# Search rounds that mask two thresholds and fold the masks on TensorE, with identity products in between

## The reference

```python
input_acts_seq = input_acts.mean(axis=1)                              # 64 x 2048
top_input_acts, top_input_idx = jax.lax.top_k(input_acts_seq, 256)
input_repr = zeros.at[brow, top_input_idx].set(top_input_acts)
process_acts = gelu(einsum('bn,pn->bp', input_repr, process_input_weights))
top_process_acts, top_process_idx = jax.lax.top_k(process_acts, 128)  # of 1024
process_weights = softmax(top_process_acts)
aggregated_value = einsum('bk,bkd->bd', process_weights, process_values[top_process_idx])
output_acts_seq = gelu(einsum('bd,od->bo', aggregated_value, output_input_weights))
top_output_acts, top_output_idx = jax.lax.top_k(output_acts_seq, 256) # of 2048
out_per_seq = einsum('bk,bkm->bm', top_output_acts, output_patterns[top_output_idx])
```

## Time and profile before

| | us |
|---|---|
| median of 3 runs | 1627.82 (1626.67 to 1629.48) |
| the profiled execution | 1629.22 |
| its span, first to last instruction | 1627.5 |
| `route` in the span | 1402 to 1627.5 |
| rounds of stage 1 | 1407.9 to 1460.5 |
| rounds of stage 2 | 1527.4 to 1579.2 |

### The profile page before, as it was taken

The page is one execution under the profiler, slowest core; times in us unless marked ns, Lnnn a source line. Parts: engine busy times, 40 slices in busy tenths (PEclk is TensorE's granted clock), DMA queues, the critical chain, the costliest instruction groups (busy, mean ns, idle before and its releaser), DMA issues. The chain is left out here.

```text
span 1627.5 us, 31837 instructions
## 1 busy us (share of the span) xinstructions
PE 1473.0 (91%) x9736; PEld 1380.4 (85%) x9736; DVE 967.6 (59%) x2424; ACT 946.6 (58%) x3359; POOL 116.9 (7%) x243
## 2 busy tenths in 40 slices
PE   5899999999999999999999999999999998774431
PEld 4799999999999999999999999999999998772330
DVE  6766655555555555555555655555566643485686
ACT  3566666666666666666666666666666654780440
POOL 0000000000000000000000000000000000000000
PEclk9999999999999999999999999999999999757555
DMA  8311111111111111111111111111110000267007
GB/s 204 80 45 45 45 44 44 42 40 40 43 44 44 44 44 44 44 44 42 39 39 40 39 40 39 39 41 44 44 44 10 10 11 10 85 210 319 0 1 316
DMA packets 53237, 99.36 MB, mean 61 GB/s; under 512 B 16720, under 2 KB 35664, under 8 KB 52176
## 3 DMA queue, kind: packets, MB, share of 16 engines
q1 hardware_dynamic: 50912, 96.91, 20.2%
q10 hardware_dynamic: 2288, 2.00, 0.6%
HBM read 73.17 MB, written 25.69 MB: 61 GB/s over the span
## 5 line engine op out<-in xcount | busy, mean ns | idle before, releaser
L625 ACT ACTIVATE ffn<-ffn 128x196 f32<-128x196 f32 x1024 | 329.5, 322 | 210.3 <-PE ffn L513 209.8
L513 PE MATMUL ffn<-x_t_hi,pat_w_hi 128*128 128x392 f32 x1024 | 361.8, 353 | 1.7 <-DVE x_t_lo L780 1.7
L513 PE MATMUL ffn<-x_t_hi,pat_w_lo 128*128 128x392 f32 x1024 | 349.5, 341 | 0.0
L513 PE MATMUL ffn<-x_t_lo,pat_w_hi 128*128 128x392 f32 x1024 | 349.0, 341 | 0.0
L716 DVE SCALAR_TENSOR_TENSOR shared<-shared,gen 98x512 f32<-98x512 f32 x64 | 44.0, 687 | 279.3 <-ACT shared L598 279.3
L513 PEld LDWEIGHTS ffn<-x_t_hi,pat_w_hi 128*128 128x128 f32 x1024 | 193.0, 188 | 6.1 <-DVE x_t_lo L780 2.0
L513 PEld LDWEIGHTS ffn<-x_t_lo,pat_w_hi 128*128 128x128 f32 x1024 | 193.6, 189 | 1.2
L625 ACT ACTIVATION_READ_ACCUMULATOR ffn<-ffn 128x1 f32 x1024 | 193.6, 189 | 0.0
L513 PEld LDWEIGHTS ffn<-x_t_hi,pat_w_lo 128*128 128x128 f32 x1024 | 192.9, 188 | 0.0
L443 PE MATMUL gen<-qkvu_w_hi,h_t_hi 128*98 128x512 f32 (+1 forms) x512 | 173.3, 338 | 2.0 <-ACT q_t L580 2.0
L443 PE MATMUL gen<-qkvu_w_hi,h_t_lo 128*98 128x512 f32 (+1 forms) x512 | 172.5, 337 | 0.0
(11 more groups left out here) (219 smaller groups left out, 2768.2 us busy)
## 6 DMA issues: line engine op xcount, KB each, us to landing
raw<-in_x_dram SPq DMA_DIRECT2D x752, 56.0 KB, 2.0
h_dram<-h SPq DMA_DIRECT2D x128, 98.0 KB
process_nat<-ocess_input_weights_dram SPq DMA_DIRECT2D x8, 1024.0 KB, 4.9
process_t<-h_dram SPq DMA_DIRECT2D x8, 896.0 KB, 11.9
out_dram<-process_t SPq DMA_DIRECT2D x8, 896.0 KB, 6.3
h_early<-h_dram SPq DMA_DIRECT2D x4, 896.0 KB, 12.3
out_dram<-h_early SPq DMA_DIRECT2D x3, 896.0 KB, 3.8
pat_nat<-_ffn_input_patterns_dram SPq DMA_DIRECT2D x1, 2048.0 KB, 15.9
```

Of the source, the lines that this page charges most:

```text
L513: last = pe.matmul(fb[f % FFN_BANKS][:, 0:T2], a[:, d, f * P:(f + 1) * P], b[:, d, :], start=n == 0, stop=n == 3 * s.halves - 1)
L625: last = act.activation(cols, cols, ACT.Gelu, accum_out=gelu_sum[:, par, at:at + 1])
```

## The change

Each round now tries two thresholds on VectorE and one on ScalarE, over all 1024 words each. VectorE no longer sums: four instructions (two thresholds, two halves of 512 words) write masks of zeros and ones in bf16 (L1305). TensorE multiplies each block of 64 mask columns with `image_sum`, now bf16, and adds the 16 blocks of a threshold in PSUM: 32 products of 64 columns a round, which wait for the four masks in turn. ScalarE's signs come in by a product of 64 columns, 63 of which are constants. VectorE then sums the 64 columns of each threshold (L1310) before it judges, so that there is one more instruction between TensorE and the judgement. In stage 2 five identity products follow each round's sums. In the ranking 24 identity products are issued once the tenth of the 16 steps is done, ahead of the turning of the ranks.

```diff
-        SHARED_AT = 5 * HALF // 8
-        reached_too = sb("reached_too", [P, 2 * HALF - SHARED_AT], BF16)
+        BLOCK = 64
+        reached_too = sb("reached_too", [P, HALF], BF16)
+        MASKED = HALF // 2
+        MASKS = 2 * HALF // MASKED
...
-        image_sum = sb("image_sum", [P, P], F32R)
+        image_sum = sb("image_sum", [P, P], BF16)
...
             def sum_halves(n):
-                tally = tallies[n % 2][:, 0:4]
                 if n == 0:
                     pe.wait_ge(numbers_made, 1)
-                if n >= 2:
-                    pe.wait_ge(judged, n - 1)
-                pe.matmul(tally, image_sum[:], offset, start=True, stop=False)
+                for m in range(2):
+                    for at in range(0, HALF, BLOCK):
+                        if at % MASKED == 0:
+                            pe.wait_ge(masked, MASKS * n + (m * HALF + at) // MASKED + 1)
+                        pe.matmul(tally[:, m * BLOCK:(m + 1) * BLOCK], image_sum[:], reached[m][:, at:at + BLOCK],
+                                  start=at == 0, stop=at == HALF - BLOCK)
                 pe.wait_ge(counted_too, n + 1)
-                pe.matmul(tally, image_minus_half[:], signs, start=False, stop=False)
-                pe.wait_ge(counted, n + 1)
-                pe.matmul(tally, image_sum[:], count, start=False, stop=True).then_inc(summed, 1)
+                pe.matmul(tally[:, 2 * BLOCK:3 * BLOCK], image_minus_half[:], signs[:],
+                          start=True, stop=True).then_inc(summed, 1)
...
+            pe.wait_ge(copied, fills + out_fills)
+            pe.wait_ge(taken, 2 * (s.k_proc // 8 - 6))
+            keep_busy(24)
             pe.wait_ge(ranks_found, 1)
...
-            pe.wait_ge(copied, fills + out_fills)
             keep_busy(5)
             place_ties(2)
...
             for n in range(STAGE, 2 * STAGE):
                 sum_halves(n)
+                keep_busy(5)
...
-                    act.activation(reached_too[:, 0:HALF], word[:], ACT.Sign, scale=-1.0, bias=tried[:, 4:5],
-                                   accum_out=signs[:, 2:3])
-                    act.activation(reached_too[:, HALF:], word[:, SHARED_AT:], ACT.Sign, scale=-1.0,
-                                   bias=tried[:, 3:4], accum_out=signs[:, 1:2]).then_inc(counted_too, 1)
+                    act.activation(reached_too[:], word[:], ACT.Sign, scale=-1.0, bias=tried[:, 4:5],
+                                   accum_out=signs[:, 0:1]).then_inc(counted_too, 1)
...
-                        for m, cols in enumerate((HALF, SHARED_AT)):
-                            last = dve.tensor_scalar(reached[m][:, 0:cols], word[:, 0:cols], tried[:, 1 + m:2 + m],
-                                                     0.0, ALU.is_ge, ALU.add, accum_out=count[:, m:m + 1])
-                        last.then_inc(counted, 1)
+                    for m in range(2):
+                        for first in range(0, HALF, MASKED):
+                            cols = slice(first, first + MASKED)
+                            dve.tensor_scalar(reached[m][:, cols], word[:, cols], tried[:, 1 + m:2 + m], None,
+                                              ALU.is_ge).then_inc(masked, 1)
...
                     dve.wait_ge(summed, n + 1)
-                    dve.tensor_scalar(passed[:], tallies[n % 2][:, 0:3], float(s.k_in), 0.0, ALU.is_ge, ALU.add,
+                    dve.reduce_sum(counts[:], tally[:, 0:3 * BLOCK].rearrange("p (m b) -> p m b", b=BLOCK),
+                                   axis=AX.X).then_inc(counted, 1)
+                    dve.wait_ge(counted, n + 1)
+                    dve.tensor_scalar(passed[:], counts[:], float(s.k_in), 0.0, ALU.is_ge, ALU.add,
                                       accum_out=found[:]).then_inc(judged, 1)
```

More of the change, by code:

```diff
@@ L945, in route @@
         ahead = sb("ahead", [P, 5])
-        blank = sb("blank", [P, 12])
-        numbers = sb("numbers", [P, 12], F32R)
-        count, signs, offset = (numbers[:, n:n + 4] for n in (0, 4, 8))
-        image_sum = sb("image_sum", [P, P], F32R)
+        blank = sb("blank", [P, BLOCK])
+        signs = sb("signs", [P, BLOCK], F32R)
+        counts = sb("counts", [P, 3])
+        image_sum = sb("image_sum", [P, P], BF16)
         image_minus_half = sb("image_minus_half", [P, P], F32R)
@@ L963, in route @@
         sums = ctx.enter_context(nc.psum_tensor("sums", [P, 512], F32))
-        tallies = [sums, turn[2]]
+        tally = turn[2]
         prod = [ctx.enter_context(nc.psum_tensor(f"rp{b}", [P, 512], F32)) for b in range(4)]
@@ L969, in route @@
         acts_turned, wide_made, chosen = sem("acts_turned"), sem("wide_made"), sem("chosen")
-        words_made, tried_made, numbers_made, counted, counted_too = sem("words_made"), sem("tried_made"), sem("numbers_made"), sem("counted"), sem("counted_too")
+        words_made, tried_made, numbers_made, counted, counted_too, masked = sem("words_made"), sem("tried_made"), sem("numbers_made"), sem("counted"), sem("counted_too"), sem("masked")
         summed, ahead_made, judged = sem("summed"), sem("ahead_made"), sem("judged")
@@ L1041, in _ @@
             pool.wait_ge(masks_made, 5)
-            pool.memset(blank[:, 9:10], (HALF - SHARED_AT) / 2)
-            pool.memset(blank[:, 10:11], HALF / 2).then_inc(masks_made, 1)
+            pool.memset(blank[:, 1:2], float(-HALF)).then_inc(masks_made, 1)
             pool.tensor_tensor(tie_share[:], other_half[:], same_image[:], ALU.subtract).then_inc(masks_made, 1)
@@ L1232, in _ @@
             act.activation(tie_signs[:], blank[:, 0:2], ACT.Copy)
-            act.activation(numbers[:], blank[:], ACT.Copy).then_inc(numbers_made, 1)
+            act.activation(signs[:], blank[:], ACT.Copy).then_inc(numbers_made, 1)
             act.activation(both_halves[:], same_image[:, 0:B].unsqueeze(2).to_broadcast([P, B, 2]), ACT.Copy)
@@ L1298, in try_three @@
                     n, at = search * ROUNDS + r, 6 * r
-                    if n == 0:
-                        dve.wait_ge(numbers_made, 1)
-                    with nc.allow_low_precision(reason="whole numbers up to 1024"):
-                        for m, cols in enumerate((HALF, SHARED_AT)):
-                            last = dve.tensor_scalar(reached[m][:, 0:cols], word[:, 0:cols], tried[:, 1 + m:2 + m],
-                                                     0.0, ALU.is_ge, ALU.add, accum_out=count[:, m:m + 1])
-                        last.then_inc(counted, 1)
+                    for m in range(2):
[3 more added lines that the diff above has]
+                                              ALU.is_ge).then_inc(masked, 1)
                     dve.tensor_scalar(ahead[:], steps[:, at + 6:at + 11], tried[:, 0:1], None,
@@ L1442, in search_steps @@
     size = 4.0 ** np.arange(KEY_ROUNDS - 1, -1, -1)
-    rounds = np.stack([0 * size, size, 2 * size, 2 * size - 0.5, 3 * size - 0.5, size], axis=1)
+    rounds = np.stack([0 * size, size, 2 * size, 3 * size, 3 * size - 0.5, size], axis=1)
     return np.tile(np.append(rounds.reshape(-1), np.zeros(6)), (P, 1)).astype(np.float32)
```

## The result

| | before | after |
|---|---|---|
| median | 1628.08 us (1626.67 to 1629.48, 6 runs) | 1622.38 us (1621.25 to 1623.62, 6 runs) |
| ratio, 95% interval | | 0.9961 [0.9951, 0.9971] |
| profiled execution, its span | 1629.2, 1627.5 us | 1622.6, 1620.9 us |
| mean granted clock | 0.938 | 0.967 |

The changed kernel is 5.7 us faster. The forecast was 9.3 us, 1618.5. The lines of the changed kernel have moved by a few: L1303 is now L1305, L1077 is L1078, L1082 is L1084, L1112 is L1114, L1150 is L1154, L1160 is L1164 and L1175 is L1180.

The account below looks back on a forecast made before the run. A chain round the engines, 3.09 us a round, was taken to bound the kernel, no engine being full. Rounds -11.8, clock falls +6.4 and ranking -3.9 gave -9.3 us: 1618.5 for the median, range 1609 to 1642.

Parts of the forecast that it names:

- its sum at the high clock: One round: 1.50 + 0.30 + 0.38 + 0.54 = 2.72 us against 3.09, saving 11.8 us in 32 rounds.
- A: In `sum_halves`, loading weights bounds the folds, 0.055 us each: 14 us slower, 1642; chance 0.13.
- B: VectorE's masks cost their upper bound, the fourth ending at 1.72 us: 7.3 us slower, 1635; chance 0.12.
- C: The clock stays low in stage 1, all 16 rounds at 3.85 us: 5.9 us slower, 1634; chance 0.07.
- the falls ahead of the first rounds: TensorE's clock falls before each stage's first round and rises after 6.6 us, 1.7 or 1.5 rounds later.
- the sum: Whole kernel: -11.8 for rounds, +6.4 for clock falls, -3.9 for the ranking, -9.3 us in all.
- an even chance: Between a stage's two searches TensorE idles some 3 us; a fall there counted half, making 1.5 falls a stage.
- Only this chain, and the ranking's end, are touched: The change affects only the 32 rounds' chain, 98.9 us of the span, and the ranking's end.
- If the clock then holds: After the ranking's 24 products, L1100, L1150 and L1160 save about 0.45, 1.8 and 1.6: 3.9 us.

Follow-up runs that it names:

- The fully filled kernel: Changed kernel with identity products around both stages' searches and ties, and throughout the ranking in place of the 24: 1610.90 us, ratio 0.9892.

## Why the prediction was right in its sign and 3.6 us too far

*Right.* The view that the chain of a round binds, not an engine, and its sum at the high clock (2.72 forecast, 2.68 measured). The masks' and the folds' prices inside their wide bounds: 0.36 for 0.349, 0.03 for 0.032, and 0.06 at the low clock for 0.054 (L1075's 32 folds in 1.89 us in the run without the five, less 0.2 for one, over 31). So rivals A and B are off; 32 products of 32 columns more a round, which raised a round by 0.47, show how near A's kind of loss lies. C is off by the granted clock, 0.91 in stage 1's window.

*Right in kind, too dear.* The falls ahead of the first rounds were there in both stages, and so were those between the searches, to which the sum gave an even chance. But the two low rounds of stage 1 took 3.55 and 3.44 us, not 3.85 (in stage 2, 3.46 and 4.21 for 4.28), and between the searches the clock was down for some 3.4 us (1432.7 to 1436.1), not 6.6: it costs 0.8 us (6.45 for 5.66) and, in stage 2, 0.2 more. So the falls cost 5.7 us in all for 6.4 (48.3 and 49.1 us for the 45.8 of a stage without one), two a stage where 1.5 were counted. With the high rounds, 0.04 us shorter each, the two stages came out 2.1 us better than the sum; that this hid part of what follows is luck.

*Wrong, the main step:* "Only this chain, and the ranking's end, are touched"; what lies behind each search was put at nothing, without a row. With the clock now up during the search there was something to lose there. The same identity products last half as long and leave TensorE idle for 1.9 and 2.5 us while VectorE places the ties, the clock falls, and the table product and the last product right behind cost 2.0 us more each. The forecast went through the low stretches ahead of each search and between the two, and not behind. Filling these two stretches brought both products back to their old length.

*Wrong, the second step:* "If the clock then holds" in the ranking. It did not: 24 products raised it at 1497.5, it fell at 1504.4, behind TensorE's waits around the ranks' transposes, rose at 1511.2 and fell again at 1514.6, ahead of most of L1164. Of 3.9 us 1.75 came. The fully filled kernel shows that the term was right for a clock that holds (3.4 to 3.9 us), and the run without the 24 that as they stand they are worth nothing that the medians show.

Open: why the clock's changes come where they do within a stretch of scattered work, and so what a single burst of products will catch, was not settled; nor why the clock stayed low in stage 2 of the kernel before with five products a round.

## What to carry to other kernels

When an edit raises the clock in one stage, walk on through the trace past that stage, and mark every idle stretch of TensorE with a product on the chain behind it: what ran at the full clock by luck before can now start low. Price the clock and the work apart, by giving the old kernel the new filling alone: here idle products without any new counting gained 7 to 9 us, and the new counting in a stage left without them lost more than it gained in the other. Count the filling at the clock that it is to hold: what fills a stretch at the low clock fills half of it at the high one. Filling paid here where it left little idle time up to the next product that matters; the lone burst of 24 moved the falls and hardly the time. And too much of it delays the chain: 18 products ahead of stage 1 cost its first round 0.9 us.

## What the runs showed of the hardware that was not expected

- In stage 2 of the kernel before with five products a round, TensorE was busy in 44.5 of 49.4 us and the granted clock stayed at 0.50; in stage 1 of the changed kernel with products around searches and ties, where it was up at the start, it stayed at 1.00 with TensorE busy in 39.8 of 46.5 us. Busy time alone doesn't tell the two apart; what does was not settled.
- With TensorE filled from its last dense part on, the clock stayed at 1.00 through both stages and the ranking, and fell at 1576.6, behind TensorE's last large product.
- Products of 32 columns in bf16, each with 128 columns of weights, start 0.025 us apart at the high clock, 64 columns 0.032 in the mean with the waits for their masks; two masks of 512 words overlap so that four are out in 1.14 us.
